# Moving attention inside TensorE's step and its consumers one step later, in a graph attention kernel

## The reference

```python
h = x @ w_lin + b_lin
dense[edge_dst, pos] = h[edge_src]            # (n, 32, 64), pos = place of the edge among the node's edges
xb = _mab(dense, dense, enc..., mask)         # attention of 32 slots to 32 slots, residual, feed-forward
xp = relu(xb @ pma_lin_w + pma_lin_b)
p  = _mab(seed, xp, pma..., mask)             # one learned query pools the 32 slots of a node
dd = _mab(p, p, dec...)
out = _layernorm(x + relu(nan_to_num(dd)))

def _mab(x, y, ...):                          # q, k, v projections of x, y, y
    o = softmax(q @ k.T / 8, masked) @ v @ out_w + out_b
    h = o + x
    return h + relu(h @ ff_w + ff_b)
```

## Time and profile before

| | |
|---|---|
| time, median of 3 runs | 4447.55 us (4446.77 to 4464.01) |
| the profiled execution's own time | 4459.52 us |
| its span | 4457.7 us |
| its mean granted TensorE clock | 0.845 of full speed |
| PE, PEld, DVE, ACT, POOL busy | 3270.3, 2035.1, 3038.5, 1656.4, 3060.7 us |
| mean busy share of the 16 DMA engines | 0.29 in the middle of the span |

### The profile page before, as it was taken

One profiled execution on the slowest core, in us unless ns is written; L12 is line 12 of the kernel. 1 busy time (PEld: TensorE's weight loads), 2 busy tenths in 40 slices (PEclk: granted clock), 3 DMA queues, 4 the chain that ended last, 5 costly groups with the idle time before them and its releaser, 6 DMA issues.

```text
span 4457.7 us, 87178 instructions
## 1 busy us (share of the span) xinstructions
PE 3270.3 (73%) x30724; PEld 2035.1 (46%) x30724; DVE 3038.5 (68%) x7088; ACT 1656.4 (37%) x2990; POOL 3060.7 (69%) x3236
## 2 busy tenths in 40 slices
PE   4777777777777777777777676777776767777777
PEld 3444444444444444444444454544444545444444
DVE  5667676767666667676666676766666667666776
ACT  2334333433333334343333343433333333333433
POOL 3777776767677667676676676766766767667771
PEclk7888888888888888888888888888888888888888
DMA  5333332222222222222232222222222222222330
GB/s 192 84 87 87 85 87 81 81 81 82 78 80 82 78 79 81 78 82 79 78 83 77 82 79 78 82 81 79 82 78 82 78 78 82 78 80 81 90 96 19
DMA packets 170667, 368.55 MB, mean 83 GB/s; under 512 B 56189, under 2 KB 109093, under 8 KB 170229
## 3 DMA queue, kind: packets, MB, share of 16 engines
q0 software_dynamic: 158032, 342.73, 27.9%
q1 hardware_dynamic: 11877, 19.76, 1.2%
q10 hardware_dynamic: 320, 0.10, 0.0%
HBM read 349.58 MB, written 16.32 MB: 82 GB/s over the span
## 4 chain that ended last, share of the span: by engine, by line
PE 47%; DVE 27%; issue 20%; POOL 4%; DVEq 1%; ACT 0%; DMA 0%; SPq 0%; ACTq 0%; POOLq 0%
PE ps L695 10%; PE ps L722 6%; PE ps L637 6%; PE ps L738 5%; PE ps L649 5%; DVE windows L951 5%; PE ps L681 4%; PE ps L708 4%; POOL gathered L545 4%; DVE xb L1090 3%; DVE h L1060 3%; DVE top L1097 2%; DVE total L1047 2%; PE ps L673 2%; DVE flags L906 2%
## 5 line engine op out<-in xcount | busy, mean ns | idle before, releaser
L545 POOL DMA_INDIRECT gathered<-node_table,idx x3125 | 2963.1, 948 | 1217.7 <-issue 894.1
L695 PE MATMUL ps<-h,ff_diag 128*128 128x512 f32 x782 | 506.1, 734 | 551.7 <-DVE h L1060 551.7
L759 ACT ACTIVATE h_apart<-ps 64x512 f32<-64x512 f32 x782 | 462.2, 591 | 989.3 <-PE ps L637 979.7
L1090 DVE SCALAR_TENSOR_TENSOR xb<-ps,cols,h 128x512 f32<-128x512 f32 x391 | 293.7, 751 | 671.9 <-PE ps L695 671.9
L637 PEld LDWEIGHTS ps<-ident,gathered 128*128 128x128 f32 x3128 | 481.2, 203 | 395.5 <-issue 395.5
L637 PE MATMUL ps<-ident,gathered 128*128 128x128 f32 x3128 | 575.3, 312 | 66.2 <-DMA gathered<-node_table,idx 66.1
L1171 DVE STREAM_TRANSPOSE probs_diag<-probs 32x512 f32<-32x512 f32 x784 | 548.9, 700 | 18.3
L722 PE MATMUL ps<-xb,pma_diag 128*128 128x512 f32 x782 | 524.5, 758 | 26.8 <-DVE xb L1090 20.6
L649 PE MATMUL ps<-probs_diag,gathered 128*64 128x128 f32 x6256 | 457.6, 290 | 91.2 <-issue 85.7
L649 PEld LDWEIGHTS ps<-probs_diag,gathered 128*64 128x64 f32 x6256 | 370.2, 169 | 264.6 <-issue 242.6
L814 ACT ACTIVATE xp<-ps,cols 128x512 f32<-128x512 f32 x391 | 267.2, 683 | 513.3 <-PE ps L722 513.2
(11 more groups left out here) (195 smaller groups left out, 3564.1 us busy)
## 6 DMA issues: line engine op xcount, KB each, us to landing
gathered<-node_table,idx POOLq DMA_INDIRECT x3125
node_table<-gathered SPq DMA_DIRECT2D x24, 384.0 KB, 2.6
out_rows<-rows SPq DMA_DIRECT2D x5, 416.0 KB
win_table<-in_dst SPq DMA_DIRECT2D x1, 1716.0 KB
win_table<-in_src SPq DMA_DIRECT2D x1, 1716.0 KB
windows<-win_table,win_idx POOLq DMA_INDIRECT x94
rows<-in_x SPq DMA_DIRECT2D x2, 640.0 KB, 5.2
rows<-in_x SPq DMA_DIRECT2D x1, 768.0 KB, 7.1
```

The lines of the kernel that those rows point to most:

```text
L545: pool.indirect_dma_start(out=gathered[:, s.slot(0, RING), t * ROW:(t + 1) * ROW], out_offset=None, in_=table, in_offset=bass.IndirectOffs ...
L695: pe.matmul(ps[:, B_FF, :], ff_diag[:, :], h2[:, s.slot(L_FF, 2), :], start=True, stop=True).then_inc(ff_ps, 1)
L759: return nc.scalar.activation(o, i, ACT.Copy)
L1090: V.scalar_tensor_tensor(xb[:, s.slot(L_FF, 2), :], ps[:, B_FF, :], c_("ff_b", P), h2[:, s.slot(L_FF, 2), :], ALU.add, ALU.max).then_inc(x ...
```

## The change

- `L_ATTEND` stays 4; h2, ff and pma get lag 5, and everything behind them one more (y is 16). The straight opening has 17 steps, the last step is 407.
- PE: attend stands after ff, before the h turn, and no longer first in the step. Attend of octet t - 4 is then used by `h2` in step t + 1.
- DVE: y rows (L1193) stand first in the step, with the statistics of them (L1196) left at the old place; maximum and subtraction (L1097, L1101), and two of the four `probs_diag` transposes, stand between `h2` and `xb`; the other two transposes stay behind `xb`.
- The search is split: counting and three of nine predicated copies at lag -6, the other six and the `idx` transpose at -4, two steps later. Window rows go from -16 to -13. POOL's own code is not changed.

```diff
-L_H2 = 4
-L_FF = 4
-L_PMA = 4
-L_BACK = 5
+L_H2 = 5
+L_FF = 5
+L_PMA = 5
+L_BACK = 6
...
-L_Y = 15
+L_Y = 16
 AT_SEARCH = -6
 AT_STRETCH = -8
-AT_ROWS = -16
+AT_SHIFT = -4
+AT_ROWS = -13
...
+    SHIFTS = 6
...
 # PE, step: the block "if s.has(L_ATTEND): ... mm.then_inc(av_ps, 1)" goes from
 # the first place to this one
                     pe.matmul(ps[:, B_FF, :], ff_diag[:, :], h2[:, s.slot(L_FF, 2), :], start=True, stop=True
                               ).then_inc(ff_ps, 1)
                 if s.has(L_ATTEND):
                     if s.slot(L_ATTEND, 2) == 0:
                         wait(pe, p_diag, s.batch(L_ATTEND) * 4 + 4)
...
 # DVE, search
             def search(u, h, buffer, at):
+                count_edges(u, h, buffer)
+                shift(u, buffer, range(BITS - 1, SHIFTS - 1, -1))
+                shift(u, buffer, range(SHIFTS - 1, -1, -1))
+                index_of(buffer, at)
...
 # DVE, step
+                if s.has_iteration(L_Y):
+                    y_rows(s)
                 if s.has_batch(L_SOFTMAX):
...
                     V.scalar_tensor_tensor(h2[:, s.slot(L_H2, 2), :], ps[:, B_AV, :], c_("bo1", P),
                                            hT[:, s.slot(L_H2, RING), :], ALU.add, ALU.add).then_inc(h2_sb, 1)
+                if s.has_batch(L_SOFTMAX):
+                    n = s.batch(L_SOFTMAX)
+                    dve.wait_ge(s_sb, n + 1)
+                    V.tensor_reduce(top[:, :].rearrange("p (h t) -> p h t", h=2), ps_slots, AX_X, ALU.max
+                                    ).then_inc(s_top, 1)
+                if s.has_batch(L_SOFTMAX):
+                    dve.wait_ge(s_top, n + 1)
+                    V.tensor_tensor(ps_slots, ps_slots,
+                                    top[:, :].rearrange("p (h t) -> p h t", h=2).unsqueeze(3).broadcast_to(
+                                        (P, 2, OCT, DEG)), ALU.subtract).then_inc(s_diff, 1)
+                if s.has_batch(L_NORM):
+                    dve.wait_ge(p_norm, n + 1)
+                    wait(dve, av_ps, s.octet(L_NORM + 2))
+                    to_diagonal(s, pr, 0, QUADS // 2)
...
                 if s.has_batch(L_NORM):
-                    dve.wait_ge(p_norm, n + 1)
-                    wait(dve, av_ps, s.octet(L_NORM + 2))
-                    to_diagonal(s, pr, 0, QUADS)
+                    to_diagonal(s, pr, QUADS // 2, QUADS)
                 if s.has_iteration(L_Y):
-                    y_rows(s)
+                    y_stats(s)
...
                 if s.has_iteration(AT_SEARCH) and (s.looped or s.at >= 8 + AT_SEARCH):
                     u = s.iteration(AT_SEARCH)
-                    for lag in (10, 9, 8, 7):
+                    par = s.slot(AT_SEARCH, RING) // OCTS_PER_IT
+                    landed(par, s.round(AT_SEARCH))
+                    count_edges(u, par, par)
+                    shift(u, par, range(BITS - 1, SHIFTS - 1, -1))
+                if s.has_iteration(AT_SHIFT) and (s.looped or s.at >= 8 + AT_SHIFT):
+                    par = s.slot(AT_SHIFT, RING) // OCTS_PER_IT
+                    shift(s.iteration(AT_SHIFT), par, range(SHIFTS - 1, -1, -1))
+                    for lag in (12, 11, 10, 9):
                         if s.has(lag):
                             dve.wait_ge(g_in[s.slot(lag, RING)], s.round(lag) * (16 * OCT) + 16 * OCT)
-                    search(u, par, par, s.slot(AT_SEARCH, PERIOD) // OCTS_PER_IT)
+                    index_of(par, s.slot(AT_SHIFT, PERIOD) // OCTS_PER_IT)
```

More of the change, by code:

```diff
@@ L57 @@
 L_ATTEND = 4
-L_H2 = 4
-L_FF = 4
-L_PMA = 4
-L_BACK = 5
[L63 to L70, removed]
-L_Y = 15
+L_H2 = 5
+L_FF = 5
+L_PMA = 5
+L_BACK = 6
+L_MASK2 = 9
+L_SEED = 9
+L_SEED_T = 10
+L_WEIGHTS = 11
+L_POOL = 12
+L_DEC1 = 13
+L_DEC2 = 14
+L_OUT = 15
+L_Y = 16
 AT_SEARCH = -6
 AT_STRETCH = -8
-AT_ROWS = -16
+AT_SHIFT = -4
+AT_ROWS = -13
 class Step:
@@ L641, in step @@
             def step(s):
[L642 to L654, removed]
                 if s.has_iteration(L_DEC1):
@@ L696, in step @@
                               ).then_inc(ff_ps, 1)
+                if s.has(L_ATTEND):
+                    if s.slot(L_ATTEND, 2) == 0:
+                        wait(pe, p_diag, s.batch(L_ATTEND) * 4 + 4)
+                    wait(pe, h2_sb, s.octet(L_ATTEND))
+                    for p in range(PAIRS):
+                        for h in range(2):
+                            lo = (2 * p + h) * ROW + 2
+                            mm = pe.matmul(ps[D * h:D * h + D, B_AV, p * P:(p + 1) * P],
+                                           gathered[:, s.slot(L_ATTEND, RING), lo:lo + ROW - 2:3],
+                                           probs_diag[:, s.slot(L_ATTEND, 4) // 2,
+                                                      OCT * s.slot(L_ATTEND, 2) + 2 * p + h, :],
+                                           start=True, stop=True)
+                    mm.then_inc(av_ps, 1)
                 if s.has(0):
@@ L929, in search, with count_edges @@
             def search(u, h, buffer, at):
+                count_edges(u, h, buffer)
+                shift(u, buffer, range(BITS - 1, SHIFTS - 1, -1))
+                shift(u, buffer, range(SHIFTS - 1, -1, -1))
+                index_of(buffer, at)
+            def count_edges(u, h, buffer):
                 dst_win = windows[:, buffer, 0:WIN]
-                src_win = windows[:, buffer, WIN:2 * WIN + DEG]
                 node = node_f[:, bass.ds(u, 1)]
@@ L948, in search, with shift @@
                 V.tensor_copy(count_slot[:, bass.ds(u * DEG, DEG)], count_turned[:, :])
-                for b in reversed(range(BITS)):
+            def shift(u, buffer, bits):
+                src_win = windows[:, buffer, WIN:2 * WIN + DEG]
+                for b in bits:
                     far = min((1 << b) - 1, WIN - (1 << b)) + DEG
@@ L953, in search, with index_of @@
                     wait_apart(dve, shifted, u * BITS + (BITS - b), dve_passed)
+            def index_of(buffer, at):
+                src_win = windows[:, buffer, WIN:2 * WIN + DEG]
                 V.transpose(idx[:, at, :], src_win[:, 0:DEG]).then_inc(idx_ready, 1)
@@ L1158, in step @@
                     u = s.iteration(AT_SEARCH)
-                    for lag in (10, 9, 8, 7):
+                    par = s.slot(AT_SEARCH, RING) // OCTS_PER_IT
[6 more added lines that the diff above has]
+                    for lag in (12, 11, 10, 9):
                         if s.has(lag):
                             dve.wait_ge(g_in[s.slot(lag, RING)], s.round(lag) * (16 * OCT) + 16 * OCT)
-                    par = s.slot(AT_SEARCH, RING) // OCTS_PER_IT
-                    landed(par, s.round(AT_SEARCH))
-                    search(u, par, par, s.slot(AT_SEARCH, PERIOD) // OCTS_PER_IT)
+                    index_of(par, s.slot(AT_SHIFT, PERIOD) // OCTS_PER_IT)
                 if s.has_iteration(AT_ROWS) and (s.looped or s.at >= 4 * DIRECT + AT_ROWS):
@@ L1194, in y_rows, with y_stats @@
                                        ).then_inc(y_ok, 1)
+            def y_stats(s):
+                m = s.iteration(L_Y)
+                row = rows[:, bass.ds(m, 1), :].rearrange("p m d -> p (m d)")
                 dve.wait_ge(y_ok, m + 1)
```

## The result

Four runs of the changed kernel have a median of 4177.77 us (4176.13 to 4178.97), four of the kernel before beside them 4448.81: the ratio on record is 0.9384, 95% interval 0.9363 to 0.9405 (the two medians alone give 0.9391). The forecast was 4160, 17.8 us or 0.4% too low. In a later group of runs the same kernel took 4175.64 against 4458.29, ratio 0.9366.

A forecast was written before the change was run, and what follows sets the result against it. POOL's gathers bound the kernel: last gather 4366.7 less 266.4 of waits gives 4100.3, landing 4102.1, tail 66.8, span 4168.9, plus 1.8 gives 4170.7, times 0.9973 gives 4160 us. Range 4145 to 4290.

The forecast's parts named there:

- POOL is the floor: POOL's 33 gathers of 1.25 us set 41.25 us for four steps, 3.3 under the present 44.55.
- Rival B: PE and DVE still hold each other up, or PE's clock drops: halfway to 44.55, 4320 us; chance 0.14.
- rival C: Denser DVE work slows every gather by 0.084 us, 2.8 in four steps: 4431 us; chance 0.03.
- rival D: Waits for gathers drop PE's clock; at half-clock share 0.8 its path is 47.1 us, 4697 in all; chance 0.03.
- Removing the stall before the pooling matmul: With the y row at the head of DVE's step, PE's 3.16 us wait before L708 goes.
- xb under 0.5 us a step: Sign of being right: DVE's xb waits for ff under 0.5 us a step, 1.7 before.
- DVE's path 37.6: DVE's own work 34.0, plus waits and loop jump: 37.6 us in four steps, between 34.9 and 38.6.
- PE's 38.5: PE's path in four steps: 33.1 us warm plus 5.4 for 31% of the time at 1.2 GHz.
- ff waiting over 2 us for h2: Sign of being wrong: PE's ff waits this long, meaning DVE's path is longer than 37.6 us.
- The ring: Eight ring slots let a late PE catch up; ring and lead of four octets swallow the loop's jump.
- Search split: Six of nine copies move at no summed DVE cost; idx comes two steps later, hidden unless steps are under 4.4 us.
- Last gather, landing, tail, discount: Last gather ends at 4100.3, landing takes 1.8, tail 66.8 (60 to 77), profile-to-median factor 0.9973.

The follow-up runs named there:

- wide score group: Eight full-width score matmuls a batch for 32 small ones, three in four scores wrong; on the kernel before: 4514.66 us, ratio 1.0126.
- y_first_8s: Kernel before with the wide score group and the y row moved to the head of DVE's step: 4171.24 us, ratio 0.9377.
- between: Kernel before with only maximum, subtraction and two of four probs_diag transposes moved between h2 and xb, chip with pauses: 5635.49 us, ratio 1.0046.
- search: Kernel before with only the search split over two steps and window rows at -13, chip with pauses: 6360.64 us, ratio 1.1336.
- y_first: Kernel before with only the y row moved to the head of DVE's step, chip with pauses: 5627.97 us, ratio 1.0037.
- lag: Kernel before with only the new lags and attend behind ff on PE, chip with pauses: 6471.7 us, ratio 1.1538.
- lag_8s: Kernel before with the wide score group, the new lags and attend behind ff, none of DVE's moves: 4409.86 us, ratio 0.9911.
- after_6g_8s: Changed kernel with the wide score group and six of each octet's eight gathers, the others stale: 4120.99 us, ratio 0.9264 of the kernel before.

## Why the prediction was right, point by point

**POOL is the floor.** Right, and its size: 41.22 us in four steps measured for 41.25. Of POOL's waits 15 name an attend, 4.6 us in all and none above 0.3, the issue gap itself. Rival B, half way, and rival C, slower gathers, are refuted by the same row: the mean gather takes 948 ns over the whole span, before and after. The Trainium skill, "SBUF — State Buffer", section "SBUF: two separate sides", is not contradicted: DVE is busy for 73% instead of 68% of the span with the same operations, and the gathers are no slower. Which of DVE's operations run in a two-port mode, no trace here shows.

**Cold PE (rival D).** It did not come. The clock went up to 0.91. The prediction's counter-argument fits, and the rows from 2021.60 show what such a wait costs where it costs something: behind 2.70 us two cold matmuls, about 1.5 us, in a step in which PE then works on. The windows show no lower clock with the gathers as the bound. The Trainium skill, "TensorE: Matmul & The Clock Gate", section "HAM oscillation — how this bites in real kernels", speaks of bursts shorter than the wait for the next DMA; here the waits for gathers are 337.3 / 187 = 1.8 us in the mean, in steps of 10.3 us, so the work between two of them is longer and its case is not met.

**Removing the stall before the pooling matmul.** Right, and worth more than the prediction says in so many words: with the wide score group the y row alone brings the whole gain (0.9377, and 0.9374 with all parts). The text made a sum for all parts together and never asked which of them covers the 3.3 us down to the floor. Whether the other parts would get there without the y row was not run; the lags alone don't.

**xb under 0.5 us a step.** Wrong: 273.0 / 391 = 0.70. It doesn't matter, as `y_first_8s` with 1.9 a step shows. Also missed: q turns wait for the gathers' DMA in 187 of 391 steps and not in most of them, a first sign that PE's path is closer to the floor than forecast.

**DVE's path 37.6, PE's 38.5.** This is the step that failed. Measured 41.3 with the wide score group, which itself puts 2 x 0.88 = 1.8 on PE in four steps. So the plain kernel's path lies, by an estimate from these, between 39.5 and the gathers' 41.25, which it doesn't pass since POOL never waits; the margin is 0 to 1.8 and not 2.8 to 3.7. Two things that the sum lacked are in the traces: the stall at the loop's edge (1.8 for 0.9), and the small decoder matmul L752 that waits 2.0 us for ACT's `hid` once in four steps with back queued behind it. How much each adds was not measured apart. The sign that the prediction names for this, ff waiting over 2 us for h2, is in the profile after: 2.3 us each in 100 steps. The ring swallows it, as forecast. Rival B's argument, that two paths of 38 which wait for each other don't come out at 38, was right; only its end, over 41.25, was not reached. With a true margin of 1.8 us or less, that the path stayed under the floor was in part luck: the sum promised twice that.

**Search split.** `idx` is never awaited by POOL in the kernel after with eight gathers (before the change it names `idx` for 11.6 us, in gaps of at most 0.3). With six, POOL waits 665.1 us for it: the later `idx` is next in line once the gathers are cheaper.

**Last gather, landing, tail, discount.** 2.4, 2.1 and 3.7 us, inside their bounds (70.5 in 60 to 77), and 10 us for a discount that was worked out from a single execution. They all go one way and make up the miss. Two small misreadings changed nothing: the longest gap before ff was 5.1 us and not 4.91, and the window with the clock of 0.59 stands behind a gap of 4.89, the one of 4.91 lying a body later.

**What stays open.** Neither `between` nor `search` ran alone on a chip where POOL is the bound, and the y row alone ran there only with the wide score group. The changed kernel with six gathers and the small scores wasn't run there either, nor was the kernel before profiled on the chip with the pauses. What the lags, the softmax work and the search bring together beside the y row is nothing measurable: 4171.24 without them is 0.9377 of the kernel before, 4179.91 with them 0.9374.

## What to carry to other kernels

Add an engine's issue gap to its busy time before you look for the bound; an engine that is 69% busy can be the floor. Then measure the distance to that floor, and ask which single stall covers it: here one moved operation of 0.28 us brought the kernel with the wide score group from 4503 to 4171 us, and the restructured pipeline beside it nothing more. Before you trust a margin under the floor, take a body of the loop with its edge in it, for every engine, and try the result on more than one chip. And when a kernel with less work comes out faster, read from its trace where: the six-gather kernel won at its two ends and nothing in its loop.

## What the hardware showed that I had not expected

- One chip runs the same program 26% slower (5612 for 4450), with the same gather time (947 ns) and PE pauses between single matmuls of a group, up to 2.5 us each and some 770 us in all. The granted clock there was 0.805 in `y_first` and 0.751 to 0.761 in the kernel before. The cause is open.
- On that chip the order of the work matters otherwise: `lag` costs 15% and `search` 13%, where `lag_8s` elsewhere is 0.9% under the kernel before.
- DVE too stands at the loop's edge: 2.77 and 2.13 us in one body of `after_6g_8s`, where the kernel before has 3.45 on PE in the earlier trace rows. That the edge is the cause is inferred from the place.
- 64 score matmuls with weights of 128 x 32 take 1.10 us, 16 with weights of 128 x 128 take 1.98: four small ones run in less time than one wide one.
